# A decoder layer on one core: projections finished in their own step, and softmax tiles handled in pairs

## The chip, the cores and the metric

One core of a Trainium2 chip runs the whole program once. The metric is the device time in microseconds; the kernel before took 2000.66 us, the median of three runs (1999.54 to 2001.34). TensorE is called PE, VectorE DVE, ScalarE ACT, GpSimd POOL and SyncE SP.

## The reference, cut to what matters

The input x has 8 batches of 512 tokens with 512 features. Self-attention, cross-attention with 16 heads and a feed-forward layer follow each other, each added to its input and normalised. The change lies in the cross-attention:

```python
q = (Q @ Wq + bq).reshape(b, len_q, H, DIM_K).transpose(0, 2, 1, 3)     # Q = x, H = 16, DIM_K = 64
k = (K @ Wk + bk).reshape(...)                                          # K = V = ctx_1024
v = (V @ Wv + bv).reshape(...)
att = jax.nn.softmax(jnp.einsum('bhqd,bhkd->bhqk', q * scale, k), axis=-1)
out = jnp.einsum('bhqk,bhkd->bhqd', att, v)
...
return out @ Wo + bo
x = _layernorm(x + _L0_xattn_ref(x, ctx_1024, ctx_1024, ...), axis=-1)
```

Each fp32 operand of a product is split in a high part of type fp32r and the rest, the low part, so that a product of full accuracy is two or three fp32r matmuls.

## The kernel before

**Groups, steps and tiles.** The cross-attention runs 16 groups, one for each batch and half of the heads (8 heads). A head has 4 tiles of 128 queries by 512 keys, so a group has 32 tiles, in 16 steps of 2. A step also holds one item of projection, or none; a step with none is called a hole here. The items are V (4 a group), K and Q (4 pairs of heads each) and O, the output projection of the group before (4). `NEXT`, `MIDDLE`, `FIRST` and `LAST` (L732 to L736) write their order out by hand: groups 1 to 14 have an item in every step (V3 K2 Q2 O0 O1 O2 K3 Q3 O3 V0+ K0+ Q0+ V1+ V2+ K1+ Q1+, where + is the next group's), group 0 has holes at steps 3, 5 and 8 (V2 V3 K2 hole Q2 hole K3 Q3 hole V0+ ...), and group 15 has them at 2, 5, 9, 11, 13, 14 and 15 (V3 K2 hole O0 Q2 hole O1 K3 Q3 hole O2 hole O3 hole hole hole). "Item step" is a step with an item, "head step" an odd one, in which a head's output is finished as well.

**The way of a tile.** PE makes the scores into a bank of `spsum` (L1280). DVE takes the row maximum (`max_tile`, L1084), ACT the exponential with its sum (`exp_tile`, L979), DVE the reciprocal (`recip`), POOL scales the row (`norm_tile`, L934). Two steps later PE transposes the tile (`turn`, L1292) into a bank of `tpsum`, ACT copies it as the high part (`pt_hi_tile`, L1008), DVE subtracts for the low part (`pt_lo_tile`, L1131), and two steps after that PE multiplies with V (`values`, L1303). `o_first` (ACT) and `o_second` (DVE) add up a head's output.

**The order on each engine.** All queues are in program order and wait on counting semaphores. In an item step PE issues the projection (12 matmuls), the scores of two tiles (4), `values` of two tiles (4) and `turn` of two tiles (8 transposes). In a hole it issues, for each of its two tiles, scores, values and turn. ACT in an item step: the item's high part (`proj_hi_part`), two exponentials, `o_first` in head steps, two `pt_hi_tile`; in a hole: exponential, `pt_hi_tile`, exponential, `pt_hi_tile`. DVE in an item step finishes the item of the step before (`finish(item_before(g, step))`, L1178: the low part of V, K or Q, or the sum for O), then two maxima, two reciprocals, `o_second`, two `pt_lo_tile`; in a hole, the first `pt_lo_tile` comes between, and the rest of the hole (`rest_of_hole`, L1146) in the step after.

**Banks.** `projp` and `tpsum` have two banks each. Projections alternate between the banks of `projp` and wait for the finish of the item two before (`bank_free`, L1236). The transposes of tile t wait for the low part of tile t - 2.

**Edges.** Before group 0 a hand-written prologue (`scalar_all` L1055, `vector_all` L1205, `tensor_all` L1341) weaves the self-attention's last normalisation with the first six items and four tiles. In group 15 DVE, ACT and POOL also normalise the first batch for the feed-forward layer (`norm_first` L1159, `add_bo` L153, `held.norm2.root` L1051), whose square root needs another table of ACT than the exponential.

Of the kernel before, what the change touches and what calls it, by code (L numbers as in the profile page):

```python
# [152 lines left out]
def add_bo(nc, held, u, c):  # L153

    x2, T = held.x2[:, u, :, :], held.norm2.T
    nc.gpsimd.wait_ge(held.y_loaded[u], 16 * c + 16)
    for i in range(T):
        nc.gpsimd.tensor_tensor(x2[:, i, :], x2[:, i, :], held.bo[:, :], ALU.add).then_inc(held.norm2.summed, 1)
# [18 lines left out]
def self_attention(nc, sc, held, banks, x, xT, ctxT, wqT, wkT, wv, wpair, biases, ident, x1, xparts, cparts, wparts,  # L177
# [22 lines left out]
    norm = Norm(sc, T, D)  # L200
# [230 lines left out]

    me.scalar_begin, me.scalar_batch, me.x1_hi_tile = scalar_begin, scalar_batch, x1_hi_tile

# [283 lines left out]
def cross_attention(nc, sc, held, banks, before, y_steps, xparts, cparts, wqparts, wkparts, wvparts, woparts, bo, WsT,  # L717
# [55 lines left out]
    def item_before(g, step):  # L773

        return SCHEDULE[g][step - 1] if step else SCHEDULE[g - 1][-1] if g else PROLOGUE[-1]
# [32 lines left out]
    def bank_of(item):  # L808

        return projp[:, NUMBER[item] % 2, :]  # L810
# [62 lines left out]
    def sync_group(g, b, h, opens, closes):  # L873
# [38 lines left out]
        if g == GROUPS - 2:  # L912
            load_x2(0)
# [41 lines left out]
    def pool_group(g):  # L955
        last = g == GROUPS - 1
        for step in range(STEPS):
            for tile in ahead(g, step):
                norm_tile(*tile)
            if step == 1 and g:  # L960
                split_out(g - 1, PAIRS - 1)
            for j in (LAST_OUT_AT if last else OUT_AT).get(step, []):
                split_out(g, j)
            if last and step == 2:
                pool.wait_ge(held.bo_loaded, 16)
                add_bo(nc, held, 0, 0)
# [41 lines left out]
    def pt_hi_tile(g, t):  # L1008
        act.wait_ge(t_mm, TILES * g + t + 1)
        wait(act, av_mm, TILES * g + t + 1 - LAG)  # L1010
        if g == t == 0:
            act.wait_ge(before.y_stored, 16 * NB)
        nc.scalar.copy(pt[:, t % LAG, HI, :], tpsum[:, t % 2, :]).then_inc(pt_hi, 1)  # L1013
# [14 lines left out]
    def scalar_group(g):  # L1028
        last = g == GROUPS - 1
        for step in range(STEPS):  # L1030
# [10 lines left out]
            else:  # L1041
# [6 lines left out]
                pt_hi_tile(g, 2 * step)  # L1048
                pt_hi_tile(g, 2 * step + 1)
            if last and step == 6:  # L1050
                held.norm2.root(nc, 0)  # L1051
# [3 lines left out]
    def scalar_all():  # L1055
# [3 lines left out]
        before.norm.root(nc, NB - 1)  # L1059
        for item in PROLOGUE[1:4]:  # L1060
# [23 lines left out]
    def max_tile(g, t):  # L1084
# [3 lines left out]
                                negate=True).then_inc(smax, 1)  # L1088

# [115 lines left out]
    def vector_all():  # L1205
# [11 lines left out]
        for pair in ((0, 1), (2, 3)):  # L1217
            for t in pair:
                max_tile(0, t)
            for t in pair:  # L1220
                recip(0, t)
# [14 lines left out]
    def bank_free(item):  # L1236

        if NUMBER[item] < 2:
            return
        other = ORDER[NUMBER[item] - 2]  # L1240
        if other[0] == "O":
# [50 lines left out]
    def turn(g, t):  # L1292
        n, k = divmod(t, T)
        head = HH * g + n
        wait(pe, pt_lo, T * head + k - 1)
        for i in range(T):
            if k == 0:
                pe.wait_ge(p_ready, T * head + i + 1)
            ins = nc.tensor.transpose(tpsum[:, k % 2, i * P:(i + 1) * P],  # L1299
# [504 lines left out]
```

## Time and profile before

| what | value |
|---|---|
| median of three runs | 2000.66 us |
| profiled execution | 2001.44 us, its span 1999.7 us, mean granted clock 0.994 |
| PE busy (matmul) | 1960.5 us, 98% of the span |
| DVE busy | 1502.5 us, 75% |
| ACT busy | 1153.3 us, 58% |
| POOL busy | 713.7 us, 36% |
| the 16 DMA engines, main queue | 48.3% |

A row of the timeline gives the start (us from the start of the span), the length, the engine, the line of the kernel, what is written and read, how many instructions are merged (x12), and in brackets the idle time before and what ended it. The granted clock is a share of TensorE's full 2.4 GHz; 0.50 is 1.2 GHz.

### The profile page before, as it was taken

The page shows a single profiled execution, that of the slowest core. Times are in us where ns is not written, and L with a number is a line of the kernel's source. Part 1 is how long each engine was busy: PE and PEld are TensorE (multiplying, and loading weights), DVE is VectorE, ACT ScalarE, POOL GpSimd, SP SyncE. Part 2 cuts the span into 40 slices and gives each one's busy share as a digit, 9 for nine tenths or more (in the row PEclk, how much of TensorE's full clock was granted, in tenths as well). Part 3 has the DMA queues.
Part 4 walks back from the last instruction along what each step waited for, and adds up shares of the span by engine and source line. Part 5 has one row for each costly group of instructions (what it writes and reads, how often), then busy time and mean ns, then how long its engine had stood idle before and what let it go on. Part 6 is the DMA issues. An engine that isn't in the chain of part 4 may idle for free. (4 is left out here: it accounts for less than half of the span.)

```text
span 1999.7 us, 29670 instructions
## 1 busy us (share of the span) xinstructions
PE 1960.5 (98%) x9856; PEld 1639.3 (82%) x9856; DVE 1502.5 (75%) x3144; ACT 1153.3 (58%) x2470; POOL 713.7 (36%) x839
## 2 busy tenths in 40 slices
PE   8999999999999999999999999999999999879998
PEld 7888888778888888888888888888888887658887
DVE  5666666777777777777777777777777777767887
ACT  5446544666766666676666667666666766532221
POOL 2222432232333333233333323333332334246663
PEclk9999999999999999999999999999999999989999
DMA  5777777764453626435452744535264454031221
GB/s 211 275 282 288 294 282 295 272 202 133 136 181 93 190 79 200 139 131 190 127 190 79 243 131 139 182 92 190 80 200 137 133 175 131 22 132 43 85 85 64
DMA packets 111223, 326.49 MB, mean 163 GB/s; under 512 B 9056, under 2 KB 9056, under 8 KB 107104
## 3 DMA queue, kind: packets, MB, share of 16 engines
q1 hardware_dynamic: 111072, 324.59, 48.3%
q8 instruction: 80, 1.31, 0.3%
q14 instruction: 71, 0.58, 0.1%
HBM read 207.12 MB, written 83.89 MB: 146 GB/s over the span
## 5 line engine op out<-in xcount | busy, mean ns | idle before, releaser
L938 POOL TENSOR_SCALAR c_prob<-c_prob,all_rden 128x512 f32<-128x512 f32 x512 | 349.2, 694 | 939.5 <-DVE all_rden L1093 938.4
L985 ACT ACTIVATE c_prob<-a_score,all_negmax 128x512 f32<-128x512 f32 x512 | 347.7, 684 | 369.3 <-DVE all_negmax L1087 368.8
L1133 DVE TENSOR_TENSOR c_pt<-a_turned,c_pt 128x512 fp32r<-128x512 f32 x512 | 330.7, 686 | 55.2 <-ACT c_pt L1013 51.5
L1087 DVE TENSOR_REDUCE all_negmax<-a_score 128x1 f32<-128x512 f32 x512 | 328.4, 682 | 6.4 <-PE a_score L1288 2.2
L1288 PE MATMUL a_score<-c_ks,c_qs 128*128 128x512 f32 x1024 | 279.1, 393 | 9.4 <-ACT c_prob L985 9.1
L1312 PE MATMUL a_av<-c_pt,c_vs 128*128 128x512 f32 x1024 | 279.4, 393 | 1.3 <-DVE c_pt L1133 1.3
L1299 PEld LDWEIGHTS a_turned<-all_ident,c_prob 128*128 128x128 f32 x2048 | 239.9, 141 | 49.6 <-DVE c_pt L1133 12.2
L1299 PE MATMUL a_turned<-all_ident,c_prob 128*128 128x128 f32 x2048 | 270.7, 274 | 9.4 <-DVE c_pt L1133 7.6
L1013 ACT CAST c_pt<-a_turned 128x512 fp32r<-128x512 f32 x512 | 274.3, 590 | 4.6 <-PE a_turned L1299 3.1
L1288 PEld LDWEIGHTS a_score<-c_ks,c_qs 128*128 128x128 f32 x1024 | 191.3, 189 | 50.8 <-ACT c_prob L985 10.1
L1093 DVE RECIPROCAL all_rden<-all_den 128x1 f32<-128x1 f32 x512 | 83.8, 164 | 198.1 <-ACT c_prob L985 198.0
L1312 PEld LDWEIGHTS a_av<-c_pt,c_vs 128*128 128x128 f32 x1024 | 193.0, 189 | 41.6 <-DVE c_pt L1133 1.7
L1275 PE MATMUL a_proj<-c_WO,c_op 128*128 128x512 f32 x768 | 192.3, 399 | 0.6 <-POOL c_op L950 0.4
L1275 PE MATMUL a_proj<-all_third_buffer,all_first_buffer 128*128 128x512 f32 x768 | 192.4, 399 | 0.0
L1275 PE MATMUL a_proj<-all_second_buffer,c_wq 128*128 128x512 f32 x768 | 191.8, 398 | 0.0
L1275 PE MATMUL a_proj<-all_first_buffer,c_wk 128*128 128x512 f32 x768 | 191.1, 398 | 0.0
L1275 PEld LDWEIGHTS a_proj<-c_WO,c_op 128*128 128x128 f32 x768 | 139.7, 188 | 32.9 <-DVE c_ks L1112 3.3
L1275 PEld LDWEIGHTS a_proj<-all_third_buffer,all_first_buffer 128*128 128x128 f32 x768 | 140.5, 189 | 27.4
L1275 PEld LDWEIGHTS a_proj<-all_second_buffer,c_wq 128*128 128x128 f32 x768 | 139.6, 188 | 27.2
L1275 PEld LDWEIGHTS a_proj<-all_first_buffer,c_wk 128*128 128x128 f32 x768 | 139.5, 188 | 26.4
L1143 DVE TENSOR_TENSOR c_osum<-a_av,c_opart 64x512 f32<-64x512 f32 x128 | 88.8, 694 | 56.9 <-ACT c_opart L1020 56.7
L1005 ACT ACTIVATE c_qs<-a_proj,all_bq 64x512 fp32r<-64x512 f32 x128 | 87.7, 685 | 55.2 <-PE a_proj L1275 53.6
(164 smaller groups left out, 2712.9 us busy)
## 6 DMA issues: line engine op xcount, KB each, us to landing
all_first_buffer<-ctxT_scratch SPq DMA_DIRECT2D x64, 512.0 KB, 7.5
c_wk<-wk_scratch SPq DMA_DIRECT2D x64, 512.0 KB, 3.8
c_wq<-wq_scratch SPq DMA_DIRECT2D x64, 512.0 KB, 4.9
all_second_buffer<-x1T_scratch SPq DMA_DIRECT2D x16, 2048.0 KB, 12.7
c_ks<-c_ks SPq DMA_DIRECT2D x128, 256.0 KB, 3.5
ctxT_scratch<-s_csp SPq DMA_DIRECT2D x8, 2048.0 KB, 7.4
c_y<-y_steps_scratch SPq DMA_DIRECT2D x16, 1024.0 KB, 5.5
y_steps_scratch<-c_y SPq DMA_DIRECT2D x15, 1024.0 KB, 5.5
```

The source lines that it names most:

```text
L938: nc.gpsimd.tensor_scalar(prob[:, n % 2, i, :], prob[:, n % 2, i, :], rden[:, n % 2, i:i + 1], 1.0, ALU.mult, ALU.mult).then_inc(p_ready, 1)
L985: nc.scalar.activation(prob[:, n % 2, i, :], spsum[:, i % 2, :], ACT.Exp, bias=negmax[:, n % 2, i:i + 1], scale=1.0, accum_out=den[:, n % ...
L1005: nc.scalar.activation(dst, bank[rows, :], ACT.Identity, bias=bias[rows, bass.ds(G * PAIRS + j, 1)], scale=1.0).then_inc(proj_hi, 1)
L1013: nc.scalar.copy(pt[:, t % LAG, HI, :], tpsum[:, t % 2, :]).then_inc(pt_hi, 1)
L1087: nc.vector.tensor_reduce(negmax[:, n % 2, i:i + 1], spsum[:, i % 2, :], AX.X, ALU.max, negate=True).then_inc(smax, 1)
L1093: nc.vector.reciprocal(rden[:, n % 2, i:i + 1], den[:, n % 2, i:i + 1]).then_inc(have_rden, 1)
L1133: nc.vector.tensor_tensor(pt[:, t % LAG, LO, :], tpsum[:, t % 2, :], as_f32(pt[:, t % LAG, HI, :]), ALU.subtract).then_inc(pt_lo, 1)
L1143: nc.vector.tensor_tensor(osum[rows, n // 2, :], opsum[DK:P, n % 2, :], opart[rows, :], ALU.add).then_inc(o_sum, 1)
L1275: ins = nc.tensor.matmul(bank_of(item), l, r, start=(k == 0 and s == m == HI), stop=(k == K - 1 and (s, m) == TERMS[-1]))
L1288: ins = nc.tensor.matmul(spsum[:, i % 2, :], qs[:, j % 2, e, i * P:(i + 1) * P], ks[:, j % 2, e, m, :], start=(m == HI), stop=(m == LO))
L1299: ins = nc.tensor.transpose(tpsum[:, k % 2, i * P:(i + 1) * P], prob[:, n % 2, i, k * P:(k + 1) * P], ident[:, :])
L1312: ins = nc.tensor.matmul(opsum[:, n % 2, :], vs[:, g % 2, k, n, :], pt[:, t % LAG, m, :], start=(k == 0 and m == HI), stop=(k == T - 1 and ...
```

## The change

On DVE an item is finished in its own step, between the maxima and the reciprocals. In item steps both tiles go through one maximum of 128x1024 elements (`max_pair`), one reciprocal of two columns (`recip_pair`), one copy (`pt_hi_pair`) and one subtraction (`pt_lo_pair`), each of which waits for both tiles. Holes stay tile by tile, but their transposes now go to the two banks of `projp`, the first tile to the bank of the next item, the second to the other one; item steps keep `tpsum`. A table of each bank's users (`BEFORE`) says what PE waits for. The normalisation of the first batch moves from group 15 to group 14 (its load from the end of group 14 to the end of group 13, `add_bo` one tile a step in steps 0 to 3, the root to step 8). A dummy exponential follows the self-attention's last square root, and the maxima of the prologue's tiles 2 and 3 come after the item Q1 is finished.

```diff
+    BANK = {item: ("proj", n % 2) for n, item in enumerate(ORDER)}
+    users = list(PROLOGUE)
+    for g, steps in enumerate(SCHEDULE):
+        for step, item in enumerate(steps):
+            pair = [("T", g, 2 * step), ("T", g, 2 * step + 1)]
+            if item:
+                users.append(item)
+                BANK.update({tile: ("turned", e) for e, tile in enumerate(pair)})
+            else:
+                made_so_far = sum(user[0] != "T" for user in users)
+                BANK.update({tile: ("proj", (made_so_far + e) % 2) for e, tile in enumerate(pair)})
+            users += pair
+    users += EPILOGUE
+    BEFORE, latest = {}, {}
+    for user in users:
+        BEFORE[user] = latest.get(BANK[user])
+        latest[BANK[user]] = user
...
+    def bank_free(user):
+        other = BEFORE[user]
+        if other is None:
             return
-        other = ORDER[NUMBER[item] - 2]
-        if other[0] == "O":
+        if other[0] == "T":
+            pe.wait_ge(pt_lo, TILES * other[1] + other[2] + 1)
+        elif other[0] == "O":
             pe.wait_ge(wo_out, T * other[1] + other[2] + 1)
...
     def turn(g, t):
-        wait(pe, pt_lo, T * head + k - 1)
+        bank_free(("T", g, t))
...
+    def pt_hi_pair(g, t):
+        act.wait_ge(t_mm, TILES * g + t + 2)
+        wait(act, av_mm, TILES * g + t + 2 - LAG)
...
+        nc.scalar.copy(pt[:, t % LAG:t % LAG + 2, HI, :], tpsum[:, :, :]).then_inc(pt_hi, 2)
...
+    def max_pair(g, t):
+        n, i = divmod(t, T)
+        dve.wait_ge(s_mm, TILES * g + t + 2)
+        nc.vector.tensor_reduce(negmax[:, n % 2, i:i + 2], spsum[:, :, :], AX.X, ALU.max, negate=True).then_inc(smax, 2)
+
+    def recip_pair(g, t):
+        n, i = divmod(t, T)
+        dve.wait_ge(p_exp, TILES * g + t + 2)
+        nc.vector.reciprocal(rden[:, n % 2, i:i + 2], den[:, n % 2, i:i + 2]).then_inc(have_rden, 2)
...
+    def pt_lo_pair(g, t):
+        dve.wait_ge(pt_hi, TILES * g + t + 2)
+        nc.vector.tensor_tensor(pt[:, t % LAG:t % LAG + 2, LO, :], tpsum[:, :, :],
+                                as_f32(pt[:, t % LAG:t % LAG + 2, HI, :]), ALU.subtract).then_inc(pt_lo, 2)
...
     def vector_group(g):
-            if not left:
-                finish(item_before(g, step))
             if item is None:
...
             else:
                 if left:
                     rest_of_hole(g, step - 1)
-                for tile in tiles:
-                    max_tile(*tile)
-                for tile in tiles:
-                    recip(*tile)
+                if tiles:
+                    max_pair(*tiles[0])
+                finish(item)
+                if tiles:
+                    recip_pair(*tiles[0])
                 if head:
                     o_second(*head)
-                pt_lo_tile(g, 2 * step)
-                pt_lo_tile(g, 2 * step + 1)
-            if last:
+                pt_lo_pair(g, 2 * step)
+            if g == GROUPS - 2:
                 norm_first(step)
...
     def scalar_group(g):
-                pt_hi_tile(g, 2 * step)
-                pt_hi_tile(g, 2 * step + 1)
-            if last and step == 6:
+                pt_hi_pair(g, 2 * step)
+            if g == GROUPS - 2 and step == 8:
                 held.norm2.root(nc, 0)
...
+    def scalar_exp_table():
+        act.wait_ge(norm.have_std, NB)
+        act.activation(unused[:, :], norm.std[:, 0:1], ACT.Exp, scale=0.0)
...
         before.norm.root(nc, NB - 1)
+        before.scalar_exp_table()
...
     def norm_first(step):
-        if step in (3, 4):
-            for i in (2 * step - 6, 2 * step - 5):
-                norm2.stats(nc, 0, i, x2)
-        if step == 6:
+        for i in {3: [0], 4: [1], 5: [2], 8: [3]}.get(step, []):
+            norm2.stats(nc, 0, i, x2)
+        if step == 8:
             norm2.variance(nc, 0)
-        if step == 7:
+        if step == 12:
             norm2.inverse(nc, 0)
-        if step in (7, 8):
-            norm2.scale(nc, x2, x2, (2 * step - 14, 2 * step - 13))
+        norm2.scale(nc, x2, x2, {12: [0], 13: [1, 2], 15: [3]}.get(step, []))
```

## Rows read from the trace of the kernel before

**Rows 1.** Timeline of PE, step starts of a middle group: start, us, work [idle before]
```profile
901.78 3.04 PE L1275 MATMUL a_proj<-c_WO,c_op 128*128 128x512 f32 x12
...
907.35 3.03 PE L1275 MATMUL a_proj<-c_WO,c_op 128*128 128x512 f32 x12
...
983.60 2.98 PE L1275 MATMUL a_proj<-all_second_buffer,c_wq 128*128 128x512 f32 x12
...
989.27 3.02 PE L1275 MATMUL a_proj<-c_WO,c_op 128*128 128x512 f32 x12
```

**Rows 2.** Timeline of DVE and ACT in step O0 of that group
```profile
907.32 1.29 DVE L1087 TENSOR_REDUCE all_negmax<-a_score 128x1 f32<-128x512 f32 x2
...
908.05 0.69 ACT L985 ACTIVATE c_prob<-a_score,all_negmax 128x512 f32<-128x512 f32 x1 [3.16 <-DVE all_negmax L1087]
...
908.73 0.68 ACT L985 ACTIVATE c_prob<-a_score,all_negmax 128x512 f32<-128x512 f32 x1
...
909.29 0.20 ACT L985 ACTIVATION_READ_ACCUMULATOR c_prob<-a_score,all_negmax 128x1 f32 x1
909.39 0.67 ACT L1020 ACTIVATE c_opart<-a_av,all_bv 64x512 f32<-64x512 f32 x1
...
909.96 1.05 ACT L1013 CAST c_pt<-a_turned 128x512 fp32r<-128x512 f32 x2
...
910.82 1.29 DVE L1133 TENSOR_TENSOR c_pt<-a_turned,c_pt 128x512 fp32r<-128x512 f32 x2
```

**Rows 3.** Groups by line and shape, ACT: busy us, mean ns
```profile
L420 ACT CAST s_pt<-a_turned 128x128 fp32r<-128x128 f32 x8 | 2.1, 265 | 0.0
```

**Rows 4.** Groups by line and shape, DVE
```profile
L544 DVE TENSOR_TENSOR s_pt<-a_turned,s_pt 128x128 fp32r<-128x128 f32 x8 | 2.2, 280 | 0.0
```

**Rows 5.** Timeline around hole 11 of group 15 and the projection after it
```profile
1742.07 1.28 DVE L1087 TENSOR_REDUCE all_negmax<-a_score 128x1 f32<-128x512 f32 x2
...
1742.79 2.99 PE L1275 MATMUL a_proj<-c_WO,c_op 128*128 128x512 f32 x12
...
1743.46 0.57 ACT L1013 CAST c_pt<-a_turned 128x512 fp32r<-128x512 f32 x1
...
1744.07 0.69 DVE L1133 TENSOR_TENSOR c_pt<-a_turned,c_pt 128x512 fp32r<-128x512 f32 x1 [0.72 <-ACT c_pt L1013]
...
1745.62 1.07 PE L1288 MATMUL a_score<-c_ks,c_qs 128*128 128x512 f32 x4
...
1746.74 1.29 DVE L1087 TENSOR_REDUCE all_negmax<-a_score 128x1 f32<-128x512 f32 x2
```

**Rows 6.** Timeline of PE, group 0: first matmuls of K2 and of Q0+
```profile
374.14 2.98 PE L1275 MATMUL a_proj<-all_first_buffer,c_wk 128*128 128x512 f32 x12
...
420.62 1.61 PE L1275 MATMUL a_proj<-all_second_buffer,c_wq 128*128 128x512 f32 x6
```

**Rows 7.** Timeline of PE in group 15: K2's first matmul; the longest stall
```profile
1677.97 3.01 PE L1275 MATMUL a_proj<-all_first_buffer,c_wk 128*128 128x512 f32 x12
...
1727.98 1.06 PE L1288 MATMUL a_score<-c_ks,c_qs 128*128 128x512 f32 x2 [4.03 <-ACT c_prob L985]
```

**Rows 8.** Timeline of DVE: the maxima of hole 13 in group 15
```profile
1751.23 1.28 DVE L1087 TENSOR_REDUCE all_negmax<-a_score 128x1 f32<-128x512 f32 x2
```

**Rows 9.** Timeline of PE: two stalls of group 0's side
```profile
362.39 1.89 PE L1288 MATMUL a_score<-c_ks,c_qs 128*128 128x512 f32 x4 [1.92 <-ACT c_prob L985]
...
407.93 0.65 PE L1299 MATMUL a_turned<-all_ident,c_prob 128*128 128x128 f32 x4 [1.43 <-DVE c_pt L1133]
```

**Rows 10.** Stretches after them: length, busy time by engine, then granted clock, DMA
```profile
362.00:367.00 5.00, 4.61 (x13) 3.42 (x14) 2.95 (x8) 3.77 (x10) 2.74 (x4) 0.66 0.94 262
407.00:411.00 4.00, 3.07 (x18) 2.66 (x19) 3.87 (x7) 0.58 (x2) 0.00 (x0) 1.00 1.07 269
```

**Rows 11.** Timeline of ACT where exp's table is loaded first
```profile
360.26 1.28 ACT L985 ACT_TABLE_LOAD   x1 [1.77 <-DVE all_negmax L1087]
```

**Rows 12.** Timeline of ACT behind the root in group 15
```profile
1717.89 1.28 ACT L985 ACT_TABLE_LOAD   x1
```

More of the change, by code:

```diff
@@ L150, in __init__, with add_bo @@
         self.softmax = [sc.sb(n, [P, 2, T]) for n in ("negmax", "den", "rden")]
-def add_bo(nc, held, u, c):
+def add_bo(nc, held, u, c, tiles=None):
     x2, T = held.x2[:, u, :, :], held.norm2.T
     nc.gpsimd.wait_ge(held.y_loaded[u], 16 * c + 16)
-    for i in range(T):
+    for i in range(T) if tiles is None else tiles:
         nc.gpsimd.tensor_tensor(x2[:, i, :], x2[:, i, :], held.bo[:, :], ALU.add).then_inc(held.norm2.summed, 1)
@@ L199, in self_attention @@
     negmax, den, rden = sc.sb("negmax", [P, T]), sc.sb("den", [P, T]), sc.sb("rden", [P, T])
-    norm = Norm(sc, T, D)
+    norm, unused = Norm(sc, T, D), sc.sb("unused", [P, 1])
     wraw, craw = sc.sb("wraw", [P, NWP, D]), sc.sb("craw", [P, K, S])
@@ L430, in scalar_batch @@
             x1_hi_tile(b, 1)
+    def scalar_exp_table():
+        act.wait_ge(norm.have_std, NB)
+        act.activation(unused[:, :], norm.std[:, 0:1], ACT.Exp, scale=0.0)
     me.scalar_begin, me.scalar_batch, me.x1_hi_tile = scalar_begin, scalar_batch, x1_hi_tile
+    me.scalar_exp_table = scalar_exp_table
     def split_x_lo(b, ks):
@@ L771, in hole @@
         return step >= 0 and SCHEDULE[g][step] is None
-    def item_before(g, step):
-        return SCHEDULE[g][step - 1] if step else SCHEDULE[g - 1][-1] if g else PROLOGUE[-1]
+    BANK = {item: ("proj", n % 2) for n, item in enumerate(ORDER)}
[15 more added lines that the diff above has]
+        latest[BANK[user]] = user
     def head_done(g, step):
@@ L806, in cross_attention, with bank_of @@
     wv_loaded, c_loaded, x_loaded, bias_ready = held.wv_loaded, held.c_loaded, held.x_loaded, held.bias_ready
-    def bank_of(item):
-        return projp[:, NUMBER[item] % 2, :]
+    def bank_of(user):
+        kind, n = BANK[user]
+        return (projp if kind == "proj" else tpsum)[:, n, :]
     def sides(e):
@@ L911, in sync_group @@
                 load_pair(wq, wqparts, nh * PAIRS + j + 1, wq_loaded)
-        if g == GROUPS - 2:
+        if g == GROUPS - 3:
             load_x2(0)
@@ L963, in pool_group @@
                 split_out(g, j)
-            if last and step == 2:
-                pool.wait_ge(held.bo_loaded, 16)
-                add_bo(nc, held, 0, 0)
+            if g == GROUPS - 2 and step < T:
+                if step == 0:
+                    pool.wait_ge(held.bo_loaded, 16)
+                add_bo(nc, held, 0, 0, [step])
     def gpsimd_all():
@@ L1012, in pt_hi_tile @@
             act.wait_ge(before.y_stored, 16 * NB)
-        nc.scalar.copy(pt[:, t % LAG, HI, :], tpsum[:, t % 2, :]).then_inc(pt_hi, 1)
+        nc.scalar.copy(pt[:, t % LAG, HI, :], bank_of(("T", g, t))).then_inc(pt_hi, 1)
+    def pt_hi_pair(g, t):
+        act.wait_ge(t_mm, TILES * g + t + 2)
+        wait(act, av_mm, TILES * g + t + 2 - LAG)
+        if g == t == 0:
+            act.wait_ge(before.y_stored, 16 * NB)
+        nc.scalar.copy(pt[:, t % LAG:t % LAG + 2, HI, :], tpsum[:, :, :]).then_inc(pt_hi, 2)
     def o_first(g, n):
@@ L1216, in vector_all @@
         before.x1_lo_tile(NB - 1, 3)
[L1217 to L1221, printed above, removed]
+        max_tile(0, 0)
+        max_tile(0, 1)
+        recip(0, 0)
+        recip(0, 1)
+        finish(PROLOGUE[5])
+        max_tile(0, 2)
+        max_tile(0, 3)
+        recip(0, 2)
+        recip(0, 3)
         for g in range(GROUPS):
@@ L1232, in cross_attention @@
     me.vector_all = vector_all
-    def bank_free(item):
-        if NUMBER[item] < 2:
+    def bank_free(user):
+        other = BEFORE[user]
+        if other is None:
             return
-        other = ORDER[NUMBER[item] - 2]
-        if other[0] == "O":
+        if other[0] == "T":
+            pe.wait_ge(pt_lo, TILES * other[1] + other[2] + 1)
+        elif other[0] == "O":
             pe.wait_ge(wo_out, T * other[1] + other[2] + 1)
@@ L1298, in turn @@
                 pe.wait_ge(p_ready, T * head + i + 1)
-            ins = nc.tensor.transpose(tpsum[:, k % 2, i * P:(i + 1) * P],
+            ins = nc.tensor.transpose(bank_of(("T", g, t))[:, i * P:(i + 1) * P],
                                       prob[:, n % 2, i, k * P:(k + 1) * P], ident[:, :])
```

2 lines of the change are left out of this document (1 added, 1 removed).

## The prediction

> **What bounds the kernel now.** I read the profile's table of busy times first: PE is busy for 98% of the span, so a change can give back at most PE's idle time and what PE loses at the lower clock, and it can cost as much as it makes PE wait. Then the timeline of PE, step by step. In a middle group the step starts at 907.35 and 983.60 are 14 steps apart, 5.446 us each, and the two steps before and behind this stretch take 5.57 and 5.67 [rows 1]. So a step has a floor of 5.45 us, and one group gives away only (5.57 + 5.67) - 2 x 5.446 = 0.35 us; PE waits there for the finish of K2, which DVE does one step late. The 14 groups without holes hold 14 x 0.35 = 5 us. The rest lies at the edges. From K2 to Q0+, group 0 takes 420.62 - 374.14 = 46.5 us [rows 6] for six steps and three holes; six steps at 5.45 and three holes at 2.7 of pure PE work would be 40.8. Group 15 takes 1751.23 - 1677.97 = 73.3 us from K2 to the maxima of hole 13 [rows 7, 8], with one stall of 4.03 us behind the root of the moved normalisation [rows 7].
>
> **The loop of DVE and ACT in an item step.** I count from M, the start of the first maximum. Before, in a head step [rows 2]: exponential at M+0.73, the second at +1.41, its sum's read-out ends at 909.49 = +2.17, `o_first` at +2.07, the copies from +2.64, the subtractions from +3.50 to +4.79. Then DVE still finishes the item.
> The pair: 512 more elements cost DVE (0.68 - 0.28) x 4/3 = 0.53 us and ACT (0.59 - 0.265) x 4/3 = 0.43 [rows 2 to 4], so `max_pair` lasts 0.68 + 0.53 = 1.21, `pt_hi_pair` 0.59 + 0.43 = 1.02. Now the first exponential starts at M+1.25, the second at +1.93, and its read-out ends 0.76 later at +2.69. The finish of a K or Q item is two operations of 512 columns, each about as long as the 0.69 of one in [rows 5], 1.4 us together; it fits between +1.14 and there, where DVE would wait anyway, so it costs nothing (0.2 where ACT's part of K2 waits for the scores). Without `o_first` the copy starts at +1.93 + 0.66 = +2.59, ends at 3.61, the subtraction starts at 3.64, and DVE can start the next maximum at 3.64 + 0.61 + 0.53 = M+4.78. With `o_first`, 0.57 more: M+5.35. The mean of the two, 5.07, is under the floor of 5.45 whatever the item. If ACT gained nothing by the pair (1.18) the mean would be 5.23, still under it. The next step's transposes need the subtraction's end, M+5.4 at the latest, and come at about M+6.1: 0.7 us of slack. So middle groups run at the floor: **-5.0 us** (ends: 0 and -5).
>
> **The holes, where I expect the loss.** A hole's transposes now write where the next projection must write. In the hole the first tile takes the next item's bank, so the whole next projection waits for that tile's low part. Before, it only waited for an item two steps back and ran under the hole's exponentials: in hole 11 the maximum starts at 1742.07 = H and the projection at 1742.79, H+0.72 [rows 5]. After, it waits for: exponential (H+0.73, as before), copy (1743.46, +1.39), subtraction (1744.07, +2.00, 0.69 long), a signal of 0.06 (an estimate; the engines start 0.02 to 0.1 behind each other in [rows 2]): **H+2.75**. A projection that starts at P lets DVE start its maximum at 1745.62 + 1.07 + 0.03 - 1742.79 = P+3.93 [rows 5]. H itself is 4.78 (5.35 in a head step) after M, as above. So from one projection over a hole to the next: 3.93 + 4.78 + 2.75 = 11.46 us, in a head step 12.03. PE has 5.45 + 2.69 = 8.14 us of work in it, and its last wait is 2.8 us long.
> Group 0, K2 to Q0+, at the full clock: 11.46 (K2) + 11.46 (Q2) + 5.45 (K3) + 12.03 (Q3) + 2 x 5.45 = 51.3 against 46.5: **+4.8**.
> Group 15, K2 to hole 13's maxima: K2 12.2 (head step, 0.2 for its late copy), O0 5.45, Q2 11.46, O1 and K3 10.9, Q3 11.46, O2 11.46, O3 3.93 + 4.78 = 8.71; sum 71.6 against 73.3: **-1.6**. The stall at the root, which lay in Q3, is gone from here and pays for the holes. What lies behind hole 13 has no further projection to hold up: 0.
>
> **The clock.** After the 1.92 us stall at 362.39 the mean granted clock from 362 to 367 is 0.66, so 5 x 0.34 = 1.7 us of PE work is lost [rows 9, 10]; the level there is 1.2 GHz. After the 1.43 us stall at 407.93 it stays at 1.00, 2.4 GHz. The 2.8 us wait in front of a projection is longer than the one that dropped it, and the lost time falls into that projection, on the path. There are seven such projections (three in group 0, four in group 15). The waits of hole and item are split among several and not every one needs to drop the clock, so I count 5 of 7: **+8.5** (ends: 0 and 7 x 1.7 = 11.9).
>
> **The rest.** Prologue: the load of exp's table, 1.28 us at 360.26 [rows 11], moves to just behind the square root. There it delays K0's and Q0's parts on ACT by 0.9, DVE's scaling and Q0's low part with them, and K1's projection, which needs that bank, by about 0.7. The stall of 1.92 shrinks to 0.6 (-1.3) with no lower clock (-1.7); Q1's finish in front of two maxima and the first transposes' wait for POOL give back 1.2. Together **-1.1** (ends: -3.5 and +1).
> The first batch's normalisation in group 14: each of three statistics and four scalings puts 0.5 to 0.7 us on DVE in steps with 0.1 to 0.67 to spare, and they are spread; the transposes' slack of 0.7 hides them. The root is not hidden: its variance is ready at about M+6.1 of step 8, V0+'s copy follows to +6.86, then exp's table is loaded for 1.28 us as at 1717.89 [rows 12] and the exponential starts at +8.15 instead of +6.70; 1.45 late less 0.7 of slack, with the inverse and its scalings 0.2 more: **+0.9** (ends: 0, as its twin in group 15 cost 4, and +4). `load_x2` is queued on SP behind the loads of the next weights, should land before POOL comes to `add_bo` at the end of step 0, and POOL, busy for 36% of the span, has room for one more operation in each of four steps. A page of the Trainium skill, ScalarE: Activation LUTs, section What ACT_TABLE_LOAD costs, puts a drain of about 1.38 us behind each load of 1.28. This trace does not agree: the exponential starts 0.02 us behind the load's end. By the page the two switches in group 14 would cost 2.8 us more and the sum would be that much later.
>
> **Sum.** -5.0 + 4.8 - 1.6 + 8.5 - 1.1 + 0.9 = +6.5 us. The profiled execution took 2001.44 us for a span of 1999.7, the runs 2000.66: I predict 2000.7 + 6.5 = **2007 us**.
>
> **Rivals.**
> 1. The clock does not drop in front of the projections (fewer than four of seven times). Then the sum is -2.0 with none and +3.1 with three: 1998.7 to 2004, no measurable change. For it: the wait of 1.43 us did no harm. Against: 1.92 did, and 2.8 is longer.
> 2. The projection is not held up, since the low part of the hole's first tile is ready early or my reading of the bank table is wrong. Then a hole and its item run at DVE's and ACT's pace, 4.78 + 4.67 (from H to the next maximum, 1746.74 - 1742.07) = 9.45 instead of 11.46, at the full clock: against the +4.8 and -1.6 above, 7 x 2.0 = 14 less. -2.0 - 14 = -16: 1985, faster. For it: this is what the separate banks seem good for, the second score no longer waits for two subtractions. Against: [rows 5] show the chain to the low part at 2.7 us from H, and PE has only its 2.7 us of hole to fill before H.
> 3. The pairs make the loop longer than the floor, in all 240 item steps: an operation over two banks that costs 0.5 us more than two single ones, on DVE or ACT, takes the mean of 5.07 over 5.45. It decides from +0.4 us a step; at +0.5 it is 240 x 0.12 = 29 us more: 2036. Against: both slopes [rows 3, 4] are flat.
>
> **Chances.** My forecast (four to seven drops) 58%; rival 1 18%; rival 2 15%; rival 3 5%; the other 4% are a normalisation or prologue that goes far better or worse. 0.2% or 4 us is what a measurement of this kernel can tell from no change. The forecast's cases lie at 2005 to 2011, nine in ten of them over 2004.7: with rival 3 and some of the rest, slower 0.60; rival 1 and the forecast's low end, same 0.22; rival 2 with a well-fitting edge, faster 0.18. The range is 1992 to 2016: rival 2's centre and rival 3 are left out, the forecast's own range is 2003 to 2012.
>
> **What would show it.** Right: middle groups of 87.1 us; PE's largest waits in front of projections behind holes, released by the subtraction, 2.8 us long, seven times, with a granted clock of 0.50 behind most; from projection to projection over a hole 11.5 us and more; no stall over 1 us in group 14. Wrong: PE entering those projections without a wait (rival 2), waits in front of scores or transposes in the middle groups (rival 3), or a granted clock that stays at 1.00 there (rival 1).

## The result, and the profile after

The changed kernel takes 2011.88 us, the median of five runs (2010.81 to 2013.0), against 2000.66 for the kernel before in the same series (1998.42 to 2002.88). The ratio is 1.0057, with a 95% interval of 1.0044 to 1.0069: **slower**, clear of the noise though by little over half a per cent, by 11.2 us where 2007 - 2000.7 = 6.3 were forecast. The profiled execution took 2011.95 us for a span of 2010.2, 10.5 more than before; its mean granted clock is 0.990 against 0.994.

**Where PE waits.** All waits of PE over the span, kernel after: engine, tile and line, what it waited for, total us, times, longest us.

```profile
PE a_proj L1322 <- DVE c_pt L1173: 16.5, 7, 2.5
PE a_score L621 <- DVE s_x1t L459: 5.6, 1, 5.6
PE a_score L1335 <- ACT c_prob L1008: 4.6, 10, 0.7
...
PE a_turned L1346 <- DVE c_pt L1178: 2.2, 4, 1.4
```

The first row is new: projections (L1322) wait for the low part of a hole's tile (L1173), seven times, up to 2.5 us.

**One of the seven.** Timeline around hole 11 of group 15, kernel after; it answers to [rows 5].

```profile
1736.64 4.60 PE L1322 MATMUL a_proj<-c_WO,c_op 128*128 128x512 f32 x12 [2.50 <-DVE c_pt L1173]
...
1742.26 1.22 DVE L1123 TENSOR_REDUCE all_negmax<-a_score 128x2 f32<-128x1024 f32 x1 [3.72 <-PE a_score L1335]
...
1744.85 1.01 ACT L1043 CAST c_pt<-a_turned 128x1024 fp32r<-128x1024 f32 x1
...
1745.97 1.22 DVE L1178 TENSOR_TENSOR c_pt<-a_turned,c_pt 128x1024 fp32r<-128x1024 f32 x1 [0.74 <-ACT c_pt L1043]
...
1747.11 1.28 DVE L1117 TENSOR_REDUCE all_negmax<-a_score 128x1 f32<-128x512 f32 x2
...
1748.50 0.58 ACT L1036 CAST c_pt<-a_proj 128x512 fp32r<-128x512 f32 x1
...
1749.11 0.69 DVE L1173 TENSOR_TENSOR c_pt<-a_proj,c_pt 128x512 fp32r<-128x512 f32 x1 [0.72 <-ACT c_pt L1036]
```

The hole's maximum starts at 1747.11 = H, the low part of its first tile ends at 1749.80, and the next projection starts at 1749.85 = H + 2.74, where it was H + 0.72 in [rows 5]. The tile that the copy at 1748.50 reads is called `a_proj`: it is in the projection's bank. The projection at 1736.64 takes 4.60 us for its 12 matmuls; undisturbed ones take 3.0.

**The clock there.** Three stretches that begin with or hold such a projection, kernel after: stretch and length, busy us of PE, PEld, DVE, ACT, POOL (instructions), granted clock, DMA share, GB/s.

```profile
384.00:389.00 5.00, 4.41 (x12) 3.52 (x13) 2.06 (x5) 1.54 (x4) 1.39 (x2) 0.66 0.60 159
417.00:422.00 5.00, 4.90 (x23) 4.05 (x24) 1.74 (x5) 1.06 (x3) 1.38 (x2) 1.00 1.01 430
1749.00:1754.00 5.00, 4.15 (x11) 3.31 (x12) 2.21 (x5) 1.79 (x5) 1.39 (x2) 0.66 0.00 0
```

A mean of 0.66 is a stretch partly at 1.2 GHz (from 1751 to 1753 the granted clock is 0.50), 1.00 is 2.4 GHz throughout. The projection of the middle stretch waited 1.86 us and was not slowed. Nor was the one of O1 in group 15, which waited 2.51 us; the other five take 4.60 to 4.62 us instead of 3.0.

**A middle group.** Timeline of PE, the steps of [rows 1] after the change.

```profile
907.00 2.98 PE L1322 MATMUL a_proj<-c_WO,c_op 128*128 128x512 f32 x12
912.43 3.01 PE L1322 MATMUL a_proj<-c_WO,c_op 128*128 128x512 f32 x12
...
988.63 3.01 PE L1322 MATMUL a_proj<-all_second_buffer,c_wq 128*128 128x512 f32 x12
994.09 1.17 PE L1322 MATMUL a_proj<-c_WO,c_op 128*128 128x512 f32 x4
```

From 907.00 to 994.09 is a whole group, 87.09 us, 16 steps at 5.44 in the mean; before it took 989.27 - 901.78 = 87.49 [rows 1].

**The pairs.** Groups by line over the whole span, kernel after: count, busy us, mean ns, idle before. The mean of the copy is 1011 ns, of the two DVE operations 1224 and 1221.

```profile
L1178 DVE TENSOR_TENSOR c_pt<-a_turned,c_pt 128x1024 fp32r<-128x1024 f32 x246 | 301.1, 1224 | 134.8 <-ACT c_pt L1043 134.8
L1123 DVE TENSOR_REDUCE all_negmax<-a_score 128x2 f32<-128x1024 f32 x246 | 300.4, 1221 | 65.2 <-PE a_score L1335 62.9
...
L1043 ACT CAST c_pt<-a_turned 128x1024 fp32r<-128x1024 f32 x246 | 248.7, 1011 | 1.4
```

**Where the 10.5 us of span went**, from the first matmul of one projection to that of another in both traces:

| stretch | before | after | difference |
|---|---|---|---|
| start to V0 of the prologue | 341.28 | 340.64 | -0.6 |
| V0 to group 0's K2 | 32.86 | 32.35 | -0.5 |
| group 0, K2 to Q0+ | 46.48 | 55.03 | +8.6 |
| group 0's Q0+ to group 14's V3 | 1164.44 | 1159.33 | -5.1 |
| group 14's V3 to group 15's K2 | 92.91 | 95.40 | +2.5 |
| group 15, K2 to O3 | 64.82 | 67.10 | +2.3 |
| O3 to the first matmul behind the attention | 20.90 | 22.93 | +2.0 |
| the rest, feed-forward | 236.0 | 237.4 | +1.4 |

### The profile page after: what moved, and what is told of

Read it like the earlier page. It is cut to its first block and busy times, and to the rows that moved or that the text cites. A ratio compares the mean times of both kernels' runs of the same rounds, so it can differ in the third digit from the quotient of the medians.

```text
span 2010.2 us, 29182 instructions
## 1 busy us (share of the span) xinstructions
PE 1962.5 (98%) x9856; PEld 1642.8 (82%) x9856; DVE 1431.9 (71%) x2406; ACT 1138.9 (57%) x2225; POOL 712.7 (35%) x839
## 5 line engine op out<-in xcount | busy, mean ns | idle before, releaser
L1178 DVE TENSOR_TENSOR c_pt<-a_turned,c_pt 128x1024 fp32r<-128x1024 f32 x246 | 301.1, 1224 | 134.8 <-ACT c_pt L1043 134.8
L1123 DVE TENSOR_REDUCE all_negmax<-a_score 128x2 f32<-128x1024 f32 x246 | 300.4, 1221 | 65.2 <-PE a_score L1335 62.9
L1346 PEld LDWEIGHTS a_turned<-all_ident,c_prob 128*128 128x128 f32 x1968 | 228.5, 140 | 36.9 <-DVE c_pt L1178 6.0
L1346 PE MATMUL a_turned<-all_ident,c_prob 128*128 128x128 f32 x1968 | 255.3, 273 | 2.3 <-DVE c_pt L1178 2.2
L1043 ACT CAST c_pt<-a_turned 128x1024 fp32r<-128x1024 f32 x246 | 248.7, 1011 | 1.4
L1322 PE MATMUL a_proj<-c_WO,c_op 128*128 128x512 f32 x768 | 196.1, 406 | 10.4 <-DVE c_pt L1173 9.7
L1322 PE MATMUL a_proj<-all_first_buffer,c_wk 128*128 128x512 f32 x768 | 193.2, 401 | 2.5 <-DVE c_pt L1173 2.5
L1322 PE MATMUL a_proj<-all_second_buffer,c_wq 128*128 128x512 f32 x768 | 193.0, 400 | 2.5 <-DVE c_pt L1173 2.5
L1322 PE MATMUL a_proj<-all_third_buffer,all_first_buffer 128*128 128x512 f32 x768 | 191.5, 398 | 2.4 <-DVE c_pt L1173 1.9
L1322 PEld LDWEIGHTS a_proj<-c_WO,c_op 128*128 128x128 f32 x768 | 143.0, 193 | 40.3 <-DVE c_pt L1173 10.6
L1322 PEld LDWEIGHTS a_proj<-all_second_buffer,c_wq 128*128 128x128 f32 x768 | 140.8, 190 | 30.0 <-DVE c_pt L1173 2.7
L1322 PEld LDWEIGHTS a_proj<-all_first_buffer,c_wk 128*128 128x128 f32 x768 | 140.5, 190 | 29.8 <-DVE c_pt L1173 2.7
L1322 PEld LDWEIGHTS a_proj<-all_third_buffer,all_first_buffer 128*128 128x128 f32 x768 | 139.6, 188 | 29.9 <-DVE c_pt L1173 2.1
L1128 DVE RECIPROCAL all_rden<-all_den 128x2 f32<-128x2 f32 x246 | 40.8, 166 | 133.7 <-ACT c_prob L1008 125.2
L1028 ACT ACTIVATE c_ks<-a_proj,all_bk 64x512 fp32r<-64x512 f32 x128 | 87.6, 685 | 35.7 <-PE a_score L1335 26.5
```

The source lines that it names most:

```text
L1028: nc.scalar.activation(dst, bank[rows, :], ACT.Identity, bias=bias[rows, bass.ds(G * PAIRS + j, 1)], scale=1.0).then_inc(proj_hi, 1)
L1043: nc.scalar.copy(pt[:, t % LAG:t % LAG + 2, HI, :], tpsum[:, :, :]).then_inc(pt_hi, 2)
L1123: nc.vector.tensor_reduce(negmax[:, n % 2, i:i + 2], spsum[:, :, :], AX.X, ALU.max, negate=True).then_inc(smax, 2)
L1178: nc.vector.tensor_tensor(pt[:, t % LAG:t % LAG + 2, LO, :], tpsum[:, :, :], as_f32(pt[:, t % LAG:t % LAG + 2, HI, :]), ALU.subtract).then ...
L1322: ins = nc.tensor.matmul(bank_of(item), l, r, start=(k == 0 and s == m == HI), stop=(k == K - 1 and (s, m) == TERMS[-1]))
L1346: ins = nc.tensor.transpose(bank_of(("T", g, t))[:, i * P:(i + 1) * P], prob[:, n % 2, i, k * P:(k + 1) * P], ident[:, :])
```

## The experiments

Each kernel differs from the changed kernel by the edit shown and was timed beside the kernel before, which took 2000.1 to 2000.7 us in these series. "Item and hole" is the time from one projection to the next with a hole between. Two theories stood: **the bank** (the hole's first tile sits in the next projection's bank, and the wait and the clock that falls behind it cost what the holes cost) and **the pairs** (operations of two banks make the loop of DVE and ACT longer and late). They don't exclude each other, so the first two edits undo one each and a third undoes both.

### The hole's first tile in another bank

```diff
-BANK.update({tile: ("proj", (made_so_far + e) % 2) for e, tile in enumerate(pair)})
+BANK.update({pair[0]: ("proj", (made_so_far + 1) % 2), pair[1]: ("turned", 1)})
```

> The changed kernel with one line of the bank table altered: in a hole the first tile's transposes go to the projection bank that the next item does not use, the second tile's to the second bank of tpsum. Theory (the held-up projections cost): no projection behind a hole waits any more; item and hole together take 9.5 to 9.9 us instead of 11.6 at seven places (7 x 2.0 = 14 us) and the clock no longer drops there (5 x 1.7 = 8.5 us), so 2011.9 - 22.5 = 1989.5 us, between 1987 and 1994. Rival (the pairs cost: DVE and ACT are late by the pair's longer operations, the projection only waits where it would have waited later anyway): the wait moves to the scores or the transposes and the time stays within 3 us of 2011.9.

Measured: 1987.62 us (1986.76 to 1988.76), ratio 0.9941 [0.9928, 0.9953], **24.3 us less** than the changed kernel. Timeline of PE in group 15 of this kernel, the projections of O2 and O3 with hole 11 between:

```profile
1718.33 2.99 PE L1322 MATMUL a_proj<-c_WO,c_op 128*128 128x512 f32 x12
...
1727.45 0.66 PE L1346 MATMUL a_turned<-all_ident,c_prob 128*128 128x128 f32 x4 [0.35 <-DVE c_pt L1178]
1727.87 3.00 PE L1322 MATMUL a_proj<-c_WO,c_op 128*128 128x512 f32 x12
```

No wait stands in front of the projection and it runs at full pace. Item and hole take 9.54 us here instead of 13.21; at five of the seven places it is 9.4 to 9.5, with a head step's item 10.1 and 10.5. The one line of the bank table turned a gain into a loss; the change's other parts with it are worth 12.5 us over the kernel before.

### Both tiles of a hole back in the transposes' own banks

```diff
-BANK.update({tile: ("proj", (made_so_far + e) % 2) for e, tile in enumerate(pair)})
+BANK.update({tile: ("turned", e) for e, tile in enumerate(pair)})
```

> The changed kernel with the holes' transposes back in the two banks of tpsum, as before the change. Theory: the projection waits for nothing, but the hole's first transposes wait for the item's pair of low parts, 4.9 us after the maximum instead of 3.0; a projection then follows 6.7 us after the item's maximum instead of 7.5, so 7 x 0.9 = 6 us less, and the longest wait is 1.9 us, so the clock falls less often (0 to 8.5 us less): 1998 to 2006 us, 2001. Rival (the bank table was needed because of the pairs, without it all is slower): over 2012 us.

Measured: 2003.66 us (2002.1 to 2006.78), ratio 1.0015 [1.0006, 1.0024]: 8.2 us less than the changed kernel, but 16 more than with the split banks. Waits of PE, then one of them on its timeline (group 0):

```profile
PE a_turned L1346 <- DVE c_pt L1178: 17.1, 12, 2.5
```

```profile
393.99 0.66 PE L1346 MATMUL a_turned<-all_ident,c_prob 128*128 128x128 f32 x4 [1.71 <-DVE c_pt L1178]
```

No projection waits at the bank any more; the wait has moved. Now the hole's first transposes wait for the subtraction of the pair of the step before (L1178). PE's waits for the low parts come to 17.1 us in twelve pieces; in the changed kernel they are 16.5 + 2.2 + 1.8 = 20.5 us, in twelve pieces too. The longest is 2.5 us and not 1.9 as expected, and four projections are still slowed (3.36 to 4.20 us), which is why most of the loss stays. So with pairs the hole's first tile is better off in a bank that neither the pair before nor the next projection uses. The remaining arrangement, the second tile alone in the next projection's bank, was not run, nor were single tiles with the hole in its own banks.

### Matmuls in front of the projection, to keep the clock

```diff
+    FILL = 9
...
+    def keep_busy(g, step):
+        pe.wait_ge(pt_lo, TILES * g + 2 * step - 2)
+        for _ in range(FILL):
+            nc.tensor.matmul(tpsum[:, 0, :], vs[:, g % 2, 0, 0, :], vs[:, g % 2, 0, 0:4, :], start=True, stop=True)
...
+                if hole(g, step - 1):
+                    keep_busy(g, step)
                 project(item)
```

> The changed kernel with nine matmuls of 512 columns added on PE in front of each projection that follows a hole; they read the group's V, write a bank of tpsum that is overwritten later, and nothing uses them. They last 9 x 0.23 = 2.05 us of a wait of 2.5 us, so the projection starts when it did. Theory (the lower clock is a cost of its own): the granted clock stays at 1.00 at the five places where it fell, 5 x 1.7 = 8.5 us less, 2003.4 us (2001 to 2006). Rival (what the lower clock takes is hidden in later waits): 2010 to 2013 us with the clock at 1.00. If the clock falls in spite of the matmuls, the run tells nothing of this.

Measured: 2002.80 us (2002.04 to 2003.54), ratio 1.0013 [1.0004, 1.0022]: 63 more matmuls, nine in front of each of the seven projections, with results that nothing uses, and the kernel is **9.1 us faster** than without them. Timeline of PE at the end of hole 11 of group 15, kernel with the filling; then, with the columns of above, the stretch with the first slowed projection and the one with this last one:

```profile
1741.06 2.33 PE L1375 MATMUL a_turned<-c_vs 128*128 128x512 f32 x9
1743.66 3.02 PE L1322 MATMUL a_proj<-c_WO,c_op 128*128 128x512 f32 x12 [0.28 <-DVE c_pt L1173]
```

```profile
384.00:389.00 5.00, 4.75 (x21) 3.59 (x20) 2.40 (x6) 2.86 (x7) 1.39 (x2) 1.00 0.78 223
1743.00:1748.00 5.00, 4.72 (x21) 3.60 (x20) 2.44 (x6) 1.61 (x4) 1.38 (x2) 1.00 0.00 0
```

The granted clock is 1.00 where it was 0.66, and the wait behind the filling is at most 0.3 us. Item and hole at the two slowed places fall from 13.24 and 13.21 to 11.63 and 11.63, the item steps of K3 in group 0 and O0 in group 15 from 7.08 to 5.46 and 5.48, and what follows O3 from 22.93 to 20.37: 9.0 us in all, 1.6 for four of them and 2.6 for the last. So the wait itself stays (11.6 is as it was, the projection can't start sooner), and **the lower clock behind it costs 9 us**. Of the 24.3 us that the split banks gave, some 15 are then the wait itself: at the full clock item and hole take 2.1 to 2.2 us less there at each of the seven places (11.61 against 9.43 at K2 in group 0).

### The pairs undone, the finish left in its step

```diff
-                pt_hi_pair(g, 2 * step)
+                pt_hi_tile(g, 2 * step)
+                pt_hi_tile(g, 2 * step + 1)
...
-                    max_pair(*tiles[0])
+                    for tile in tiles:
+                        max_tile(*tile)
                 finish(item)
...
-                    recip_pair(*tiles[0])
+                    for tile in tiles:
+                        recip(*tile)
...
-                pt_lo_pair(g, 2 * step)
+                pt_lo_tile(g, 2 * step)
+                pt_lo_tile(g, 2 * step + 1)
```

> The changed kernel with the four pair operations of item steps split into two single ones again; the item is still finished in its own step, the bank table stays. Theory (the middle groups gain by the finish in its own step, not by the pairs; the pairs make the low part later): middle groups stay at 87.1 us, and in front of a hole DVE is free 3.9 us after the first maximum instead of 4.8, so the seven held-up projections start 0.9 us earlier: -6 us, 2006 us (2002 to 2008). Rival (the middle groups gained by the pairs): they go back to 87.5 us or more, +5 us, which eats the gain: 2011 us.

Measured: 1994.09 us (1991.92 to 1995.98), ratio 0.9970 [0.9958, 0.9981], 17.8 less than the changed kernel and 12 less than was expected. Timeline of PE and DVE in group 15 of this kernel, the projection of O2, its maxima, those of hole 11, the projection of O3:

```profile
1726.38 3.03 PE L1326 MATMUL a_proj<-c_WO,c_op 128*128 128x512 f32 x12 [2.16 <-DVE c_pt L1174]
1729.91 1.29 DVE L1118 TENSOR_REDUCE all_negmax<-a_score 128x1 f32<-128x512 f32 x2 [1.62 <-PE a_score L1339]
1733.80 1.28 DVE L1118 TENSOR_REDUCE all_negmax<-a_score 128x1 f32<-128x512 f32 x2
1736.54 1.66 PE L1326 MATMUL a_proj<-c_WO,c_op 128*128 128x512 f32 x6 [1.71 <-DVE c_pt L1174]
```

From the item's maxima to the hole's it is 1733.80 - 1729.91 = 3.89 us; with the pair it was 1747.11 - 1742.26 = 4.85. From a projection's start to its maxima it is 3.53, since the first maximum need not wait for the second tile's scores; the pair was put at 3.93, and it is 4.03 at O1 of the changed kernel, from 1714.12 to 1718.15. From the hole's maxima to the projection it is 2.74 both times: that is the bank. Item and hole take 10.2 us here instead of 11.6. The middle groups stay at 87.09 us, so the finish alone brings the 5 us there and the pairs nothing. Group 14 takes 87.09 too, where it took 89.95, and the clock fell behind only two of the seven waits. By stretches the two profiles differ by 0.5 us from V0 to K2, 6.4 in group 0, 2.9 in group 14, 3.9 in group 15, 3.1 behind O3 and the rest, 0.8, at the start and in the feed-forward. The expectation had DVE free 0.9 us earlier at each hole, and it was (4.85 - 3.89 = 0.96). It left out the rest: group 14, three drops of the clock fewer, the earlier first maximum, and what lies behind O3.

### Both undone

The two edits above together, the split banks and single tiles.

> Both changes that helped, together: the hole's tiles in the unused projection bank and in tpsum, and single operations instead of pairs; the finish stays in its own step. Theory (the two costs are separate: the held-up projection, and the pair's later low part, which also makes the 2.8 us of stalls in group 14): DVE is free 0.9 us earlier in front of seven holes, so 6 us, and group 14 is back at 87.1: 1987.6 - 6 - 2.9 = 1979 us (1976 to 1982), faster than both kernels. Rival (with the banks mended the pairs cost nothing more in the holes): 1985 us.

Measured: **1976.53 us** (1976.26 to 1977.62), ratio 0.988 [0.9867, 0.9894], 35.4 less than the changed kernel and 24 less than the kernel before: the fastest of all. Timeline of PE, O2 and O3 of group 15:

```profile
1710.93 3.00 PE L1326 MATMUL a_proj<-c_WO,c_op 128*128 128x512 f32 x12
...
1719.49 2.77 PE L1326 MATMUL a_proj<-c_WO,c_op 128*128 128x512 f32 x11
```

8.56 us for item and hole, near the 8.14 of PE's own work. The four kernels make a square:

| | next projection's bank shared | split banks |
|---|---|---|
| pairs | 2011.88 | 1987.62 |
| single tiles | 1994.09 | 1976.53 |

The bank costs 24.3 us with pairs and 17.6 without; the pairs cost 17.8 with the shared bank and 11.1 without. Both theories hold, and the two costs don't simply add: the bank costs 6.7 us more with pairs than without. At least in the profiled executions the clock fell behind five of the seven waits with pairs and behind two with single tiles, and three drops at 1.6 us make up most of it. About 1 us of what the pairs cost lies in the feed-forward layer and is no part of them, as told below.

### The normalisation back in group 15

```diff
-            if g == GROUPS - 2 and step == 8:
+            if last and step == 6:
                 held.norm2.root(nc, 0)
...
-            if g == GROUPS - 2:
-                norm_first(step)
+            if last:
+                norm_first(step)
```

(`norm_first`'s steps, `add_bo` and `load_x2` are as in the kernel before, too.)

> The changed kernel with the first batch's normalisation back in group 15 as before (load, add_bo, statistics, root, inverse, scaling). Theory (a shift from one group to the other): group 14 becomes 2.8 us shorter (87.1), group 15 gets back a stall of 2 to 4.5 us at the root: between -1 and +2, 2011 to 2014 us. Rival (the move is a loss by itself, since group 15 waits anyway at its holes and the root would hide there): 2009 us, all 2.8 us come back.

Measured: 2015.32 us (2014.85 to 2018.3), ratio 1.0082 [1.0068, 1.0095], 3.4 more than the changed kernel and a little over what was expected. Timeline of PE, group 15 of this kernel:

```profile
1735.00 1.22 PE L1336 MATMUL a_score<-c_ks,c_qs 128*128 128x512 f32 x2 [2.56 <-ACT c_prob L1007]
...
1741.42 1.89 PE L1323 MATMUL a_proj<-c_WO,c_op 128*128 128x512 f32 x7 [1.03 <-DVE c_pt L1172]
```

Group 14 gets its 2.85 us back, and group 15 pays: from K2 to O3 it takes 1753.06 - 1679.79 = 73.3 us instead of 67.1. The root's stall is the old one of [rows 7], 2.56 us instead of 4.03, and the projection of O1 waits 3.71 us at the bank instead of 2.51. So the move is worth 3.4 us with the banks as they are.

### The finish at the start of the next step, with pairs

```diff
             left = hole(g, step - 1)
+            if not left:
+                finish(item_before(g, step))
...
                     max_pair(*tiles[0])
-                finish(item)
```

(In the prologue `finish(PROLOGUE[5])` goes to the next step, too.)

> The changed kernel with its pairs, but the item finished at the start of the next step, as before. Theory (the pairs alone would make DVE's and ACT's loop longer than PE's step): a group's loop is 8 x 5.35 + 8 x 4.78 plus finishes of 8 x 0.6 and 8 x 1.5, 97.8 us against 87.1, so middle groups take 98 us and the whole some 150 us more, 2160 us. Rival (the finish was never on the loop; it only moved the wait for K2): middle groups at 87.5 us, 2017 us.

Measured: 2235.36 us (two runs, 2234.76 and 2235.96), ratio 1.1173 [1.1152, 1.1193]. The direction was foreseen, 75 us of the size were not. Waits of PE, then three maxima on the timeline of DVE in a middle group:

```profile
PE a_turned L1350 <- DVE c_pt L1182: 77.6, 117, 1.0
PE a_proj L1326 <- DVE c_qs L1156: 27.7, 58, 0.9
PE a_proj L1326 <- DVE c_ks L1156: 20.1, 58, 0.6
```

```profile
900.07 1.22 DVE L1127 TENSOR_REDUCE all_negmax<-a_score 128x2 f32<-128x1024 f32 x1
906.08 1.22 DVE L1127 TENSOR_REDUCE all_negmax<-a_score 128x2 f32<-128x1024 f32 x1
911.52 1.21 DVE L1127 TENSOR_REDUCE all_negmax<-a_score 128x2 f32<-128x1024 f32 x1
```

With a finish in front of the pair's maximum a step takes up to 6.0 us and more: a middle group is 100.9 us long, 6.3 a step in the mean, where 5.44 is the floor. PE waits for DVE at the transposes (117 times) and at the projection's bank (116 times), each in about half of the steps, so DVE sets the pace. Why 100.9 and not the 97.8 expected was not followed up. It shows what the pair needs: without the finish moved behind the maximum, it is far over the floor. With single tiles the finish could stand in either place ([rows 1] against the kernel with single tiles: 87.49 and 87.09).

### No dummy exponential in the prologue

```diff
         before.norm.root(nc, NB - 1)
-        before.scalar_exp_table()
         for item in PROLOGUE[1:4]:
```

> The changed kernel without the dummy exponential behind the square root; exp's table is loaded in front of the first real one again. Theory (the preload takes a stall and a spell of lower clock out of the prologue): the first exponential is 0.6 us later, PE waits 2 us there and the clock falls for 1.7 us of work: +2 to +3.5, 2014.5 us. Rival (the preload only moves the wait into K1's projection): within 1 us of 2011.9.

Measured: 2012.67 us (2009.47 to 2013.73), ratio 1.0055 [1.0041, 1.0068]: by its time not told from the changed kernel's 2011.88. The profile is finer. Timeline of PE, the kernel without the dummy, then the changed kernel:

```profile
362.24 1.85 PE L1334 MATMUL a_score<-c_ks,c_qs 128*128 128x512 f32 x4 [1.89 <-ACT c_prob L1008]
363.90 4.08 PE L1321 MATMUL a_proj<-all_third_buffer,all_first_buffer 128*128 128x512 f32 x12
```

```profile
361.31 1.40 PE L1335 MATMUL a_score<-c_ks,c_qs 128*128 128x512 f32 x4 [0.64 <-ACT c_prob L1008]
362.54 2.90 PE L1322 MATMUL a_proj<-all_third_buffer,all_first_buffer 128*128 128x512 f32 x12
```

The stall of [rows 9] is back, and with it the lower clock in V2's projection (4.08 us instead of 2.90). From V0 to K2 it is 33.70 us without the dummy, 32.35 with it and 32.86 in the kernel before. So the table loaded early gives 1.35 us, half of what was expected, and the rest of the change takes 0.84 of it back. Of this the pairs are 0.5: V3's step takes 5.06 us in the changed kernel, 4.54 in the kernel before and 4.52 with single tiles. The remaining 0.35 may be the order in which Q1's finish comes ahead of two maxima; no run tries that alone.

## Why the prediction was right

The sum had the sign and the main mechanism, and its size was short by 4.9 us; 2011.9 is the upper end of the forecast's own range of 2003 to 2012. Point by point, predicted and measured in the stretches of the table above:

**Middle groups, -5.0: right, -5.1** for thirteen groups, 0.39 each and not 0.35. The single tiles showed that the reason given is also the right one, the finish in its own step; the pair, 1.22 and 1.01 us long as worked out (1.21 and 1.02), stays under the floor but brings nothing.

**Holes and clock, +4.8 - 1.6 + 8.5 = +11.7: right, +12.9.** The shared bank was read rightly from the code: H + 2.74 measured, H + 2.75 predicted; 11.61 us for item and hole, 11.46 predicted; the last wait is 2.5 us, 2.8 predicted. The clock fell behind five of the seven waits, as counted, and gave 9.1 us back when the waits were filled, 8.5 predicted. The price of a drop was read from a row, but nothing was given for the count of five, and that it came out is luck: the wait of 2.15 us at O0 dropped the clock and the 2.51 at O1 did not. Behind hole 13 the prediction put nothing; 2.0 us were lost from O3 on, where the clock at O3's projection is a part. The square adds a point that the prediction lacked. Its 4.78 us from an item's maximum to the hole's hold the pair's lateness, but the loss was put down to the banks alone, and the pair was called free because the mean step stays under the floor. Around a hole, where the loop of DVE and ACT is on the path, it costs 1.0 to 1.4 us each time at the full clock (0.4 once), and 11 to 18 us over the kernel.

**The normalisation in group 14, +0.9: too small, the term that was mis-sized.** The sign of being right "no stall over 1 us in group 14" was missed, too. The stretch lost 2.5 us although its middle steps gained 0.35, so the move costs 2.85 there. Timeline of ACT, DVE and PE in group 14, kernel after:

```profile
1635.68 1.21 DVE L1123 TENSOR_REDUCE all_negmax<-a_score 128x2 f32<-128x1024 f32 x1
...
1639.30 1.28 ACT L92 ACT_TABLE_LOAD   x1
...
1641.90 0.20 ACT L92 ACTIVATE all_norm_std<-all_norm_variance 128x4 f32<-128x4 f32 x1 [1.33 <-DVE all_norm_variance L84]
...
1642.60 1.28 ACT L1008 ACT_TABLE_LOAD   x1
...
1643.90 0.69 ACT L1008 ACTIVATE c_prob<-a_score,all_negmax 128x512 f32<-128x512 f32 x1
...
1647.19 1.22 DVE L1178 TENSOR_TENSOR c_pt<-a_turned,c_pt 128x1024 fp32r<-128x1024 f32 x1 [0.41 <-ACT c_pt L1043]
...
1648.47 1.09 PE L1346 MATMUL a_turned<-all_ident,c_prob 128*128 128x128 f32 x8 [1.41 <-DVE c_pt L1178]
```

The exponential starts 8.22 us after the maximum of 1635.68 (8.15 predicted), so the chain was right up to there. Behind it the subtraction came some 0.3 later and the transposes were due 0.2 earlier than the slack of 0.7 supposed: the wait is 1.41 us, and the step of K0+ took 7.19 us instead of 5.44, 1.75 more. The other 1.1 are three steps near the statistics (put at nothing) and the scalings (put at 0.2): K3 5.80, K1+ 5.89, Q1+ 5.76. DVE had room for them in the mean, and not at the place in the step where they stand. Both go with single tiles (87.09), so the slack that failed is the one that the pair had used up.

The exponential again starts 0.02 us behind the table's load (1642.60 + 1.28 = 1643.88). The drain of about 1.38 us that the Trainium skill, ScalarE: Activation LUTs, section What ACT_TABLE_LOAD costs, puts behind each load is not seen in this trace either, nor a gap ahead of the load, which starts 0.01 us behind the end of ACT's copy (1642.59).

**Prologue, -1.1: -0.5.** The prediction had 2.3 us of gain by the early table and 1.2 of loss by the order and a wait for POOL. The early table gave 1.35, and the loss was 0.84, of which 0.5 are pairs that the prediction had not counted here.

**Not foreseen: +1.4 in the feed-forward layer**, whose code is the same. It is the clock: the first 20 us of it, kernel before, then kernel after, with the columns of above.

```profile
1779.00:1799.00 20.00, 16.33 (x66) 13.26 (x67) 15.54 (x36) 7.65 (x19) 11.38 (x10) 0.74 0.37 120
```

```profile
1788.00:1808.00 20.00, 16.20 (x60) 12.92 (x61) 14.26 (x31) 7.65 (x19) 11.37 (x10) 0.66 0.39 120
```

The mean granted clock is 0.08 lower over 20 us, 1.6 us of work. The experiments fall into the same two kinds: with 0.74 in this stretch (single tiles, both undone, holes in their own banks) the layer takes 235.7 to 236.5 us, with 0.66 to 0.68 (split banks, filling, normalisation back, no dummy) 237.3 to 237.5. Why the low clock lasts longer in some is not known. The start, 0.6 us earlier, varies from kernel to kernel by as much (340.2 to 341.3 us) with the same code.

Of the rivals, the first (the clock stays) is refuted by the stretches at 0.66. The second (the projection isn't held) fell by the seven waits, but its time, 1985, is nearly what the split banks measured, 1987.6: it described the kernel that this one could have been. The third (pairs over the floor) fell in the middle groups, and that the pairs cost time was half true at the holes; its 240 steps with pairs are 246 (x246 above).

## What to carry to other kernels

When two kinds of short-lived data share a buffer with an engine's next large job, ask at which moment the last reader frees it and what that job would have run under: one entry of a bank table was worth 24 us here. An operation over both tiles gained nothing anywhere in this kernel, whose middle groups are bound by PE; where latency binds, it costs the wait for the second tile at its start and the first tile's early end at its finish. Whether it pays where DVE or ACT is the limit was not shown. A mean step under the floor proves it for the steady loop only, so work out the edges apart.

## What the runs showed of the hardware

- Waits of 2.15 to 2.51 us in front of a projection were followed by a stretch at 1.2 GHz in five of six cases, and one of 1.86 us was not. In the kernel with single tiles one of two waits of 2.16 us in group 15 was followed by it (4.60 us for the projection) and the other was not (3.03 us), so the length of the wait alone does not decide. Each drop cost about 1.6 us of PE work, and nine further matmuls ahead of the projection (2.33 us in hole 11's case) avoided it.
- An operation over two banks lasts 1.22 us on DVE and 1.01 us on ACT; two single ones in a row take 1.29 and 1.05 [rows 2]. The pair saves 0.07 and 0.04 us and delays the first tile by 0.5 (1.22 against the 0.69 of one subtraction in [rows 5]).
- A square root's table load runs ahead of what its instruction waits for: in group 14 it starts at 1639.30 and lasts 1.28 us, and the variance is ready only at 1641.9, so that half of the switch costs ACT nothing in this place.
